# Pointwise product on split, masked h; the last two boxes on VectorE; x3 in one buffer

## The chip, the cores and the metric

The kernel runs on one core of a Trainium2 chip. The metric is device time in microseconds for one execution of the whole program; smaller is better. A core has five engines that run their own instruction streams side by side: TensorE (PE), VectorE (DVE), ScalarE (ACT), GpSimd (POOL) and SyncE (SP), which here only starts DMAs. They wait for each other through semaphores.

## What is computed

Thirty-two images of 256 channels and 28 x 28 positions go through four residual layers, all in fp32 at the interface:

```
x = x + L0(_gn(x))   # mixture of 8 pointwise convolutions, weights by sparsemax of a gate
x = x + L1(_gn(x))   # depthwise 3x3, batch norm, relu, prune; pointwise, batch norm, relu, prune
x = x + L2(_gn(x))   # attention over tokens with squared, normalised q and k
x = x + L3(_gn(x))   # 3x3 box filter with weights 1/9
```

`_gn` is a group norm with 32 groups. The part that the change touches first is in L1: after the depthwise convolution `h = _prune(h, 4.0)` sets a whole channel of an image to zero when its largest value is below 4, and then the pointwise product `pw_w @ h` mixes the 256 channels. The part touched second is L3: each output position is x3 plus the sum over its 3 x 3 neighbourhood of the normalised x3 (scaled by 1/9, zero outside the image).

## The kernel before

The 256 channels lie as J = 2 halves of 128 partitions; one half of an image is a tile 128 x 784. The program is a software pipeline over images. `run` calls each engine's `step(t)` for t = -1 to 36 (t = 8 to 29 as a hardware loop of pairs), and in a step seven images are in work at once, named by their stage: Z = t+1 (load), A = t (layer 0), B = t-1 (depthwise), C_ = t-2 (prune and pointwise), D = t-3 (queries, keys), E = t-4 (attention out, x3), F = t-5 (box). Order within a step is written out by hand for each engine; it is the order of calls in that engine's `step`. All waits are on semaphores counted per image. A full step, with every stage active, is one period of the pipeline; there are 28 steps from t = 4 to t = 31 that end with an image in stage A.

The order on **PE** in a step is: `value_out(E)`, key norms, `attention_weights(E)` (L503, L506), `gate_logits(A)` (L448), `attention_out(E)` (24 products of L457), `mix_experts(A)` (L585), `keys(D)` (L536, L539), `queries(D)` (24 of L457), transposes (L471), `pointwise(C_)` (8 of L457), `query_sums` (L555), `mixed_conv(A)` (L598), `query_scales` (L567), `keys_x` (L610), `key_sums` (L484), `group_means` (L441). The helper `conv_tile` issues all 128 x 392 products from L457. Products on two "parts" use a split: a value is stored as a rounded fp32r high part and the fp32r remainder, and `by_parts` multiplies high by high, high by low and low by high, so three products stand for one. `pointwise` doesn't use the split: it multiplies plain fp32 `pw_masked` by plain fp32 `h`.

The order on **ACT** around the change: relu of the depthwise result (`relu_h`, L1097), split of xn2, `sum_over_h` (L1106, which finds whether a channel reaches 4), `normalise_x3(F)` (L1013), `scaled_mix(A)` (L1029, waits for `mix_experts`), the second `sum_over_h`, then `square_k` (L1133, seven tiles) interleaved with four sums over the next input (`x0_sum`, L1042), `square_q` (L1142), `copy_tokens` (L1059), `fourth_powers_q` (L1151), `relu_y` and `sum_over_y` (L1123, L1115), `q_norms` (L1158), the sums of squares (L992), `q_high` (L1050) and `kx_high` (L1164).

The order on **DVE**: group norm scales, `q_low(E)` (L858), one depthwise tap, `attention_weights_low(E)` (L871), the sparsemax, `x2_low(D)` (L878), `make_x3(E)` (L840), two taps, `h_mask(C_)` (L811), `box_row_sums(F)` (L851, L853), `reciprocal_sums(D)` (L884, waits for all of `square_k`), nine taps (L803), `q_scales(D)` (L895, waits for `q_norms`), `make_x2`, `make_x1`, `scale_q`, the last six taps, `kx_low`.

**POOL** normalises x1 into `xpad` (L1256), and then `mask_weights` (L1280) multiplies the pointwise weights by the image's channel mask; PE's `pointwise` waits for that. Then `add_rows(F)` adds the box to the result in memory: SP has stored x3 of the image to `out`, and POOL issues three DMAs that accumulate `row_sums`, shifted by 0, 1 and 2 rows, into it, one after the other:

```
for n in range(BOX_ROWS):
    if n:
        pool.wait_ge(rows_added[n - 1].of(F), rows_added[n - 1].at(F))
    rows = row_sums[:, :, n:n + H, :].rearrange("p j h w -> p j (h w)")
    pool.dma_start(out_dram[F.times(1)], rows, accum_op=ALU.add).then_inc(rows_added[n].of(F), 16)
```

`box_row_sums(F)` overwrites `row_sums` and so waits for the DMAs of the image before. x3 has two buffers, so `make_x3(E)` waits for the store and the normalising of the image two before.

Of the kernel before, what the change touches and what calls it, by code (L numbers as in the profile page):

```python
# [5 lines left out]
ALU = mybir.AluOpType  # L6
# [6 lines left out]
P = 128  # L13
# [19 lines left out]
STAGES = 7  # L33

# [15 lines left out]
class Image:  # L50
# [21 lines left out]
    @property  # L72
    def active(self):

        return self.pair is not None or 0 <= self.offset < IMAGES

# [36 lines left out]
def build(nc, x, gate_wT, gate_b, expert_rows, mix_pattern, dw_w, channel_params, pw_wT, w_qk, b_qk, w_vT, w_ln, group_mean, ident, out):  # L113
    with ExitStack() as ctx:
# [18 lines left out]
        pw_sb = sb("pw_sb", [P, J, C])  # L133
# [24 lines left out]
        pw_masked = sb("pw_masked", [P, J, C])  # L158
# [12 lines left out]
        q_parts = sb("q_parts", [P, 2, J, HW], F32R)  # L171
        x3 = sb("x3", [P, 2, J, HW])
# [4 lines left out]
        wqk_raw = x3[:, 0].rearrange("p j n -> p (j n)")[:, 0:J * 2 * C].rearrange("p (j n) -> p j n", j=J)  # L177
        wv_ln = x3[:, 1].rearrange("p j n -> p (j n)")[:, 0:2 * J * C].rearrange("p (w j n) -> p w j n", w=2, j=J)
# [80 lines left out]
        pw_masked_ready = sig("pw_masked_ready", J)  # L259
# [40 lines left out]
        row_step = sig("row_step", 2)  # L300

# [10 lines left out]
        def row_operands(n):  # L312
# [5 lines left out]
                    (sums, sums, x3pad[:, :, 1:1 + H, 2:2 + W])][n]  # L318

# [3 lines left out]
        def run(eng, step):  # L323
# [32 lines left out]
            (pw_sb[:], pw_wT.rearrange("(j p) o -> p j o", p=P)),  # L356
# [5 lines left out]
        def _(sp):  # L362
# [9 lines left out]
            def step(t):  # L372
                Z, E = t + 1, t - 4
# [11 lines left out]
            for last in (Image(None, IMAGES - 2), Image(None, IMAGES - 1)):  # L385
# [6 lines left out]
        def _(pe):  # L392
# [261 lines left out]
        def _(dve):  # L654
# [15 lines left out]
            def setup_weights():  # L670
# [25 lines left out]
                for n, (bn, bias) in enumerate(((bn1_sb, dwb_sb), (bn2_sb, pwb_sb))):  # L696
# [4 lines left out]
                    did(nc.vector.tensor_tensor(bn_shift[:, n, :], bn_tmp[:, n, :], bn[:, 1, :], ALU.add))  # L701
                parts_of(wqk, wqk_raw)
# [85 lines left out]
            def depthwise(B, turns):  # L788

                for j, tap in TAP_TURNS[turns]:  # L790
                    if tap == 0:
                        dve.wait_ge(xpad_ready.sem, xpad_ready.at(B, j + 1))
                        if (B - 2).active:
                            dve.wait_ge(pw_mm.sem, pw_mm.at(B - 2))
# [11 lines left out]
            def h_mask(C_):  # L806

                dve.wait_ge(h_over_sum.sem, h_over_sum.at(C_))
                if (C_ - 1).active:
                    dve.wait_ge(pw_masked_ready.sem, pw_masked_ready.at(C_ - 1))  # L810
                nc.vector.tensor_scalar(hmask[:], h_over[:], 0.0, None, ALU.is_gt).then_inc(hmask_step.sem, 1)  # L811

# [534 lines left out]
```

## Time and profile before

| | us |
|---|---|
| median of 3 runs (lowest to highest) | 1646.85 (1644.88 to 1647.62) |
| the profiled execution, its own time | 1646.53 |
| its span in the trace | 1644.9 |
| PE busy | 1517.3 (92%) |
| DVE busy | 1296.9 (79%) |
| ACT busy | 1186.2 (72%) |
| POOL busy | 304.0 (18%) |

The span is what the trace covers; the 1.6 us between it and the execution's own time lie around the program. "Busy" counts only work, not waits. An engine's share is an average over the filling of the pipeline (to about 145 us), the full steps (to about 1446 us) and the draining. In the trace's rows a number behind "idle" or in square brackets is the time that the engine stood still just before the instruction, with what ended it. PE and PEld are TensorE's products and its weight loads, which overlap.

### The profile page before, as it was taken

Reading aid. Unit: us, or ns where it says so; the run is one execution under the profiler, and the core shown is the slowest. Engines: PE = TensorE matmul, PEld = TensorE weight load, DVE = VectorE, ACT = ScalarE, POOL = GpSimd, SP = SyncE. Lnnn points to the kernel's source line nnn. Section 1 sums busy time; section 2 is a strip of 40 time slices with the busy share of each in tenths; the row PEclk is TensorE's granted clock in tenths of the full one; section 3 lists DMA queues with packets and bytes.
Section 4 is the critical chain, followed back from the end, with each engine's and each line's share of the span. In section 5 each row is a group of like instructions: output and inputs, shape, how many; then the busy total and the mean of one; then the engine's idle time right before and its main releaser. Section 6 shows DMA issues by size and latency. Waiting matters only on the chain.

```text
span 1644.9 us, 27605 instructions
## 1 busy us (share of the span) xinstructions
PE 1517.3 (92%) x9282; PEld 1219.7 (74%) x9282; DVE 1296.9 (79%) x2339; ACT 1186.2 (72%) x2440; POOL 304.0 (18%) x238
## 2 busy tenths in 40 slices
PE   4469999999999999999999999999999999999850
PEld 2247787888887877878887877888877878878750
DVE  5758888888988888888888888889888888885430
ACT  3357777887777778877787778877787778776530
POOL 1100022222221121222221221222211221211001
PEclk8679999999999999999999999999999999999975
DMA  4001044434334444433334444333434444333435
GB/s 144 22 20 40 21 99 99 98 62 94 82 80 95 78 98 98 82 74 86 89 79 90 86 98 98 73 84 78 89 87 78 98 98 79 67 72 67 80 72 96
DMA packets 47172, 132.70 MB, mean 81 GB/s; under 512 B 3857, under 2 KB 4881, under 8 KB 47122
## 3 DMA queue, kind: packets, MB, share of 16 engines
q0 software_dynamic: 26112, 77.08, 28.8%
q1 hardware_dynamic: 20914, 54.98, 8.8%
q8 instruction: 28, 0.46, 0.1%
q14 instruction: 22, 0.18, 0.0%
q10 hardware_dynamic: 96, 0.00, 0.0%
HBM read 29.29 MB, written 102.76 MB: 80 GB/s over the span
## 4 chain that ended last, share of the span: by engine, by line
PE 90%; DVE 4%; DMA 2%; ACT 2%; issue 1%; POOLq 0%; ACTq 0%; DVEq 0%
PE conv_ps L457 35%; PE tile_ps L610 12%; PE tile_ps L539 10%; PE conv_ps L598 9%; PE small_ps L585 4%; PE tile_ps L484 4%; PE tile_ps L471 3%; PE tile_ps L567 3%; PE tile_ps L506 3%; DMA out<-row_sums 2%; PE tile_ps L503 2%; PE tile_ps L536 2%; PE tile_ps L555 2%; DVE h L803 1%; PE small_ps L448 1%
## 5 line engine op out<-in xcount | busy, mean ns | idle before, releaser
L803 DVE SCALAR_TENSOR_TENSOR h<-xpad,dw_sb,h 128x784 f32<-128x784 f32 x512 | 492.5, 1029 | 0.0
L1270 POOL DMA_DIRECT2D out<-row_sums x96 | 115.6, 1204 | 491.9 <-DMA out<-row_sums 411.2
L610 PE MATMUL tile_ps<-k,xT 112*128 112x256 f32 x896 | 201.4, 383 | 0.0
L1280 POOL TENSOR_SCALAR pw_masked<-pw_sb,hmask 128x256 f32<-128x256 f32 x64 | 118.4, 1857 | 385.4 <-DVE hmask L811 377.0
L610 PEld LDWEIGHTS tile_ps<-k,xT 112*128 112x128 f32 x896 | 171.9, 193 | 22.2
L539 PE MATMUL tile_ps<-wqk,xn_parts 128*112 128x256 f32 x1344 | 187.4, 294 | 0.0
L992 ACT ACTIVATE junk<-x 128x784 bf16<-128x784 f32 x192 | 162.8, 851 | 26.7 <-DVE x L830 17.5
L457 PE MATMUL conv_ps<-h,pw_masked 128*128 128x392 f32 x512 | 176.3, 498 | 5.5 <-issue 5.5
L598 PE MATMUL conv_ps<-x,mixed 128*128 128x392 f32 (+1 forms) x512 | 176.5, 498 | 2.2 <-ACT mixed L1029 1.1
L539 PEld LDWEIGHTS tile_ps<-wqk,xn_parts 128*112 128x112 f32 x1344 | 169.5, 175 | 0.1
L457 PE MATMUL conv_ps<-xn_parts,w_out 128*128 128x392 f32 x768 | 151.0, 345 | 0.0
L1256 POOL TENSOR_SCALAR xpad<-x,gn_rs 128x784 f32<-128x784 f32 x64 | 64.4, 1008 | 455.2 <-DVE gn_rs L727 455.2
L457 PEld LDWEIGHTS conv_ps<-h,pw_masked 128*128 128x128 f32 x512 | 96.1, 193 | 70.6 <-issue 9.4
L598 PEld LDWEIGHTS conv_ps<-x,mixed 128*128 128x128 f32 x512 | 95.8, 192 | 68.9 <-issue 6.6
L457 PE MATMUL conv_ps<-q_parts,attn_parts 128*128 128x392 f32 x768 | 145.3, 345 | 0.0
L457 PE MATMUL conv_ps<-xn_parts,wqk 128*128 128x392 f32 x768 | 142.7, 341 | 0.0
L457 PEld LDWEIGHTS conv_ps<-q_parts,attn_parts 128*128 128x128 f32 x768 | 135.9, 188 | 0.4 <-DVE attn_parts L871 0.3
L457 PEld LDWEIGHTS conv_ps<-xn_parts,wqk 128*128 128x128 f32 x768 | 135.7, 188 | 0.0
L457 PEld LDWEIGHTS conv_ps<-xn_parts,w_out 128*128 128x128 f32 x768 | 134.5, 188 | 0.0
L1042 ACT ACTIVATE junk<-x 128x784 bf16<-128x784 f32 x128 | 109.2, 854 | 1.1 <-issue 1.1
L1142 ACT ACTIVATE q<-conv_ps,bq_col 128x784 f32<-128x784 f32 x64 | 58.6, 915 | 50.4 <-PE conv_ps L457 50.2
L1133 ACT ACTIVATE k<-tile_ps 112x256 f32<-112x256 f32 x224 | 84.2, 381 | 8.0 <-PE tile_ps L539 7.9
(141 smaller groups left out, 2631.8 us busy)
## 6 DMA issues: line engine op xcount, KB each, us to landing
out<-row_sums POOLq DMA_DIRECT2D x96, 784.0 KB, 7.1
x<-x SPq DMA_DIRECT2D x32, 784.0 KB, 5.5
out<-x SPq DMA_DIRECT2D x32, 784.0 KB, 3.5
expert_sb<-expert_rows SPq DMA_DIRECT2D x8, 256.0 KB, 5.1
x<-w_qk SPq DMA_DIRECT2D x1, 512.0 KB
x<-w_vT SPq DMA_DIRECT2D x1, 256.0 KB
x<-w_ln SPq DMA_DIRECT2D x1, 256.0 KB
pw_sb<-pw_wT SPq DMA_DIRECT2D x1, 256.0 KB
```

Source lines behind the costliest of these rows:

```text
L457: mm = nc.tensor.matmul(conv_ps[:, 2 * j + a, 0:HALF], wt[:, half(j)], act[:, a * HALF:(a + 1) * HALF], start=(first and i == 0), stop=(la ...
L484: mm = nc.tensor.matmul(tile_ps[strip * SUB:(strip + 1) * SUB, KSUM_BANK, cols], weight.to_broadcast([TOK, SUB]), keys[:, m, :], start=(m ...
L539: mm = nc.tensor.matmul(dst, xn2_parts[:, u, i, m * TOK:(m + 1) * TOK], wqk[:, v, i, C:2 * C], start=False, stop=(i == J - 1 and u == 1))
L585: mm = nc.tensor.matmul(small_ps[s * SUB:(s + 1) * SUB, :], mix_w[:, g, :], expert_sb[:, g, s, :], start=(g == 0), stop=(g == PACKED - 1), ...
L598: mm = nc.tensor.matmul(conv_ps[:, 2 * j + a, 0:HALF + more], mixed[:, i * C + j * P:i * C + (j + 1) * P], x0[:, A.odd, i, a * HALF:(a + 1 ...
L610: mm = nc.tensor.matmul(tile_ps[:, KX_BANK, i * C:(i + 1) * C], xT[:, m, half(i)], k2[:, m, :], start=(m == 0), stop=(m == M - 1))
L803: ins = nc.vector.scalar_tensor_tensor(acc, view, scalar, acc, ALU.mult, ALU.add)
L992: nc.scalar.activation(junk[:, j * HW:(j + 1) * HW], source[:, j, :], ACT.Square, accum_out=gn_in[:, layer, 2 + j:3 + j]).then_inc(gn_sums ...
L1042: nc.scalar.activation(junk[:, j * HW:(j + 1) * HW], x0[:, Z.odd, j, 0:HW], func, accum_out=gn_in[:, 0, first + j:first + j + 1]).then_inc ...
L1133: nc.scalar.activation(k2[:, m, :], tile_ps[0:TOK, K_BANK[m // 2], m % 2 * C:(m % 2 + 1) * C], ACT.Square, accum_out=k_sum[:, m:m + 1]).th ...
L1270: pool.dma_start(out_dram[F.times(1)], rows, accum_op=ALU.add).then_inc(rows_added[n].of(F), 16)
L1280: nc.gpsimd.tensor_scalar(pw_masked[:, j, :], pw_sb[:, j, :], hmask[:, j:j + 1], 0.0, ALU.mult, ALU.add).then_inc(pw_masked_ready.sem, 1)
```

## The change

The pointwise product now goes by parts. The weights `pw_parts` are split once, in the setup on DVE (two more operations of `parts_of`). For each image ACT's new `h_high` makes the masked high part of h, and DVE's new `h_low` the masked remainder; POOL's `mask_weights` is gone. The parts of h live in the buffer that held those of q. In the last two images (`TAIL = 2`) the box is added on DVE by `box_in_tail` and stored by SP, half by half, in place of the store and the three accumulating DMAs. x3 is one buffer; x3 of the last image lies in x1's buffer. `normalise_x3` moves ahead of the first `sum_over_h` on ACT.

```diff
@@ SP, step
-                if E.active:
+                if E.active and not E.in_tail:
                     sp.wait_ge(x3_ready.sem, x3_ready.at(E))
-                    sp.dma_start(out_dram[E.times(1)], x3[:, E.odd]).then_inc(stored.of(E), 16)
+                    sp.dma_start(out_dram[E.times(1)], x3[:]).then_inc(stored.of(E), 16)
+                if F.in_tail:
+                    for j in range(J):
+                        sp.wait_ge(tail_step.sem, tail_step.at(F - (IMAGES - TAIL), 5 * (j + 1)))
+                        sp.dma_start(out_dram[F.offset][:, j, :], x3_of(F)[:, j, :]).then_inc(tail_stored, 16)
@@ PE
             def pointwise(C_, halves):
-                pe.wait_ge(h_ready.sem, h_ready.at(C_))
-                pe.wait_ge(pw_masked_ready.sem, pw_masked_ready.at(C_))
+                pe.wait_ge(h_lo.sem, h_lo.at(C_))
                 for j in halves:
                     wait_free((C_ - 1, q2_ready, j + 1), (C_ + 1, x1_ready, j + 1))
-                    conv_tile(j, [(pw_masked[:, i, :], h[:, C_.odd, i, :]) for i in range(J)]).then_inc(pw_mm.sem, 1)
+                    conv_tile(j, by_parts(pw_parts, h_parts)).then_inc(pw_mm.sem, 1)
@@ DVE
+                parts_of(pw_parts, pw_raw)
                 parts_of(wqk, wqk_raw)
...
+            def h_low(C_):
+                for j in range(J):
+                    dve.wait_ge(h_hi.sem, h_hi.at(C_, j + 1))
+                    nc.vector.scalar_tensor_tensor(h_parts[:, 1, j, :], h[:, C_.odd, j, :], hmask[:, j:j + 1],
+                                                   h_parts[:, 0, j, :].bitcast(F32), ALU.mult,
+                                                   ALU.subtract).then_inc(h_lo.sem, 1)
...
             def make_x3(E):
-                if (E - 2).active:
-                    dve.wait_ge(stored.of(E - 2), stored.at(E - 2))
-                    dve.wait_ge(x3pad_ready.sem, x3pad_ready.at(E - 2))
+                if (E - 1).active and not (E - 1).in_tail:
+                    dve.wait_ge(stored.of(E - 1), stored.at(E - 1))
                 for j in range(J):
+                    if (E - 1).active:
+                        dve.wait_ge(x3pad_ready.sem, x3pad_ready.at(E - 1, j + 1))
                     dve.wait_ge(attn_mm.sem, attn_mm.at(E, j + 1))
...
+            def box_in_tail(F):
+                s, turn = tail_step, F - (IMAGES - TAIL)
+                for rows in rows_added:
+                    last = Image(None, IMAGES - TAIL - 1)
+                    dve.wait_ge(rows.of(last), rows.at(last))
+                for j in range(J):
+                    pad, rows, done = x3pad[:, j], row_sums[:, j], 5 * j
+                    inner, out = pad[:, 1:1 + H, 1:1 + W], x3_of(F)[:, j, :]
+                    dve.wait_ge(x3pad_ready.sem, x3pad_ready.at(F, j + 1))
...
@@ DVE, step
                 if C_.active:
                     h_mask(C_)
-                if F.active:
+                if F.in_tail:
+                    box_in_tail(F)
+                elif F.active:
                     box_row_sums(F)
+                if C_.active:
+                    h_low(C_)
@@ ACT
+            def h_high(C_):
+                act.wait_ge(hmask_step.sem, hmask_step.at(C_))
+                if (C_ - 2).active:
+                    act.wait_ge(attn_mm.sem, attn_mm.at(C_ - 2))
+                for j in range(J):
+                    nc.scalar.activation(h_parts[:, 0, j, :], h[:, C_.odd, j, :], ACT.Identity,
+                                         scale=hmask[:, j:j + 1]).then_inc(h_hi.sem, 1)
@@ ACT, step
-                if C_.active:
-                    sum_over_h(C_, 0)
                 if F.active:
                     normalise_x3(F)
                 if C_.active:
+                    sum_over_h(C_, 0)
                     relu_h(C_, 1)
...
                     sum_over_h(C_, 1)
+                    h_high(C_)
@@ POOL, step
-                if C_.active:
-                    mask_weights(C_)
-                if F.active:
+                if F.active and not F.in_tail:
                     add_rows(F)
```

The five operations of `box_in_tail` for a half are left plus middle column, plus right column (both into `row_sums`), upper plus middle row, plus lower row (both into the padded tile), and x3 plus that sum; each waits for the one before.

How the instructions of ACT stand in a full step of the loop, from the relu of the second half of h on. Names are tiles: `over,h_over` is the sum of `sum_over_h`, `mixed` the scaled expert weights, `hq_parts` the new parts of h, `k,k_sum` the squared keys, `junk,gn_in` a sum over the input. Before:

```order
L1097 ACTIVATE h<-h,bn_shift,bn_scale 128x784
L1029 ACTIVATE mixed<-small_ps,gn_rs 128x256 x2
L1105 REGISTER_ALU
L1106 ACTIVATE over,h_over<-h,below 128x784
L1132 REGISTER_ALU
L1133 ACTIVATE k,k_sum<-tile_ps 112x256 x2
```

With the change:

```order
L1157 ACTIVATE h<-h,bn_shift,bn_scale 128x784
L1087 ACTIVATE mixed<-small_ps,gn_rs 128x256 x2
L1165 REGISTER_ALU
L1166 ACTIVATE over,h_over<-h,below 128x784
L1171 REGISTER_ALU
L1175 ACTIVATE hq_parts<-h,hmask 128x784 x2
L1201 REGISTER_ALU
L1202 ACTIVATE k,k_sum<-tile_ps 112x256 x2
```

Two operations on 128 x 784 now stand between the second sum over h and the first squared key, behind a wait for DVE's mask.

The end of DVE's stream, from x3 of the last image (`x,gn_in<-conv_ps,b_out,x`) on. Before:

```order
L840 SCALAR_TENSOR_TENSOR x,gn_in<-conv_ps,b_out,x 128x784 x2
L851 TENSOR_TENSOR row_sums<-x3pad 128x2x784
L853 TENSOR_TENSOR row_sums<-row_sums,x3pad 128x2x784
L713 COPY gn_avg<-small_ps 128x16
```

With the change:

```order
L871 SCALAR_TENSOR_TENSOR x,gn_in<-conv_ps,b_out,x 128x784 x2
L885 TENSOR_TENSOR row_sums<-x3pad 128x784
L887 TENSOR_TENSOR row_sums<-row_sums,x3pad 128x784
L890 TENSOR_TENSOR x3pad<-row_sums 128x28x28
L892 TENSOR_TENSOR x3pad<-x3pad,row_sums 128x28x28
L894 TENSOR_TENSOR x<-x,x3pad 128x784
```

The five rows stand twice for image 30, and twice again for image 31 behind the group norm's last rows; the two whole-image row sums of each of these images are gone.

## Rows read from the trace of the kernel before

**Rows 1.** Busy time by engine in a stretch of full steps; columns as in the heading.

```profile
core 0: us, PE busy (x) PEld busy (x) DVE busy (x) ACT busy (x) POOL busy (x), PEclk, DMA share, GB/s
440.00:1000.00 560.00, 560.00 (x3491) 453.14 (x3490) 481.76 (x854) 445.06 (x921) 116.86 (x86) 1.00 0.40 87
```

**Rows 2.** The chain that ended last: start us, duration us, what.

```profile
144.89 0.33 PE small_ps L441 x2
...
710.22 4.42 PE conv_ps L457 x24
...
722.35 4.30 PE conv_ps L457 x24
...
727.96 5.27 PE conv_ps L457 x16
...
1445.82 0.33 PE small_ps L441 x2
```

**Rows 3.** Timeline of DVE and of PE's weight loads where `attention_out` begins.

```profile
755.58 0.87 DVE L871 SCALAR_TENSOR_TENSOR attn_parts<-tile_ps,k_inv,attn_parts 128x256 fp32r<-128x256 f32 x2
...
756.52 0.19 PEld L457 LDWEIGHTS conv_ps<-q_parts,attn_parts 128*128 128x128 f32 x1
```

**Rows 4.** Timeline of ACT in one full step.

```profile
718.31 0.38 ACT L1133 ACTIVATE k<-tile_ps 112x256 f32<-112x256 f32 x1
...
724.59 0.92 ACT L1142 ACTIVATE q<-conv_ps,bq_col 128x784 f32<-128x784 f32 x1 [0.21 <-PE conv_ps L457]
726.69 0.91 ACT L1142 ACTIVATE q<-conv_ps,bq_col 128x784 f32<-128x784 f32 x1 [1.18 <-PE conv_ps L457]
727.50 2.29 ACT L1059 ACTIVATE xT<-tile_ps,k_rec 112x256 f32<-112x256 f32 x6
...
735.75 0.32 ACT L1158 ACTIVATE q_norm<-tile_ps 128x196 f32<-128x196 f32 x1
```

**Rows 5.** Timeline of DVE in the same step.

```profile
718.41 0.17 DVE L811 TENSOR_SCALAR hmask<-h_over 128x2 f32<-128x2 f32 x1 [0.43 <-ACT over L1106]
...
724.42 0.17 DVE L884 TENSOR_SCALAR k_eps<-k_sum 112x7 f32<-112x7 f32 x1 [1.94 <-ACT k L1133]
...
736.10 0.27 DVE L895 TENSOR_SCALAR q_alpha<-q_norm 128x196 f32<-128x196 f32 x1 [2.56 <-ACT q_norm L1158]
```

**Rows 6.** Groups by line and shape, ACT, 300 to 1400 us: busy, mean ns.

```profile
L998 ACT ACTIVATE xn<-x,gn_rs 128x784 f32<-128x784 f32 x46 | 45.5, 1036 | 0.7
...
L1092 ACT CAST xn_parts<-xn 128x784 fp32r<-128x784 f32 x46 | 36.7, 845 | 10.1 <-PE conv_ps L457 10.1
```

**Rows 7.** The page's group of depthwise taps on DVE.

```profile
L803 DVE SCALAR_TENSOR_TENSOR h<-xpad,dw_sb,h 128x784 f32<-128x784 f32 x512 | 492.5, 1029 | 0.0
```

**Rows 8.** Timeline of DVE, ACT and POOL in the drain.

```profile
1454.25 1.86 DVE L878 TENSOR_TENSOR xn_parts<-xn,xn_parts 128x784 fp32r<-128x784 f32 x2 [1.03 <-ACT xn_parts L1092]
...
1589.69 0.08 DVE L840 DVE_READ_ACCUMULATOR x<-conv_ps,b_out,x 128x1 f32 x1
...
1593.22 0.16 DVE L713 COPY gn_avg<-small_ps 128x16 f32<-128x16 f32 x1
...
1594.76 1.97 ACT L1013 ACTIVATE x3pad<-x,box_rs 128x784 f32<-128x784 f32 x2 [0.73 <-DVE box_rs L735]
...
1635.95 1.20 POOL L1270 DMA_DIRECT2D out<-row_sums  x1 [6.29 <-DMA out<-row_sums]
```

**Rows 9.** DMA issues on the page: count, KB each, us to landing.

```profile
out<-row_sums POOLq DMA_DIRECT2D x96, 784.0 KB, 7.1
...
out<-x SPq DMA_DIRECT2D x32, 784.0 KB, 3.5
```

**Rows 10.** Timeline of DVE in the setup.

```profile
31.38 0.69 DVE L665 CAST wqk<-x 128x1024 fp32r<-128x1024 f32 x1
32.11 1.23 DVE L666 TENSOR_TENSOR wqk<-x,wqk 128x1024 fp32r<-128x1024 f32 x1
```

**Rows 11.** Timeline of PE and POOL in the fill, at the first pointwise product.

```profile
77.30 3.12 POOL L1280 TENSOR_SCALAR pw_masked<-pw_sb,hmask 128x256 f32<-128x256 f32 x2 [8.45 <-issue]
...
80.52 7.88 PE L457 MATMUL conv_ps<-h,pw_masked 128*128 128x392 f32 x16 [5.49 <-issue]
```

**Rows 12.** Timeline of PE in the drain, two waits of the same length.

```profile
1479.02 2.98 PE L567 MATMUL tile_ps<-q_alpha,idn 128*128 128x196 f32 x8 [3.44 <-DVE q_alpha L900]
...
1524.26 1.59 PE L567 MATMUL tile_ps<-q_alpha,idn 128*128 128x196 f32 x8 [3.44 <-DVE q_alpha L900]
```

More of the change, by code:

```diff
@@ L75, in active, with in_tail @@
         return self.pair is not None or 0 <= self.offset < IMAGES
+    @property
+    def in_tail(self):
+        return self.pair is None and IMAGES - TAIL <= self.offset < IMAGES
     @property
@@ L318, in row_operands, with x3_of, image_rows @@
                     (sums, sums, x3pad[:, :, 1:1 + H, 2:2 + W])][n]
+        def x3_of(E):
+            return x1[:, E.odd] if E.pair is None and E.offset == IMAGES - 1 else x3[:]
+        def image_rows(tile):
+            return tile.rearrange("p (h w) -> p h w", w=W)
         def conv_banks(j):
@@ L378, in step @@
                     sp.dma_start(x0[:, Z.odd, :, 0:HW], x_dram[Z.times(1)]).then_inc(x_loaded.of(Z), 16)
-                if E.active:
+                if E.active and not E.in_tail:
                     sp.wait_ge(x3_ready.sem, x3_ready.at(E))
                     hold(sp, "sp")
-                    sp.dma_start(out_dram[E.times(1)], x3[:, E.odd]).then_inc(stored.of(E), 16)
+                    sp.dma_start(out_dram[E.times(1)], x3[:]).then_inc(stored.of(E), 16)
[3 more added lines that the diff above has]
+                        sp.dma_start(out_dram[F.offset][:, j, :], x3_of(F)[:, j, :]).then_inc(tail_stored, 16)
             run(sp, step)
-            for last in (Image(None, IMAGES - 2), Image(None, IMAGES - 1)):
+            sp.wait_ge(tail_stored, 16 * J * TAIL)
+            for last in (Image(None, IMAGES - TAIL - 2), Image(None, IMAGES - TAIL - 1)):
                 sp.wait_ge(stored.of(last), stored.at(last))
@@ L1007, in normalise_x3 @@
             def normalise_x3(F):
[L1009 removed]
+                if (F - 1).in_tail:
+                    act.wait_ge(tail_step.sem, tail_step.at(F - 1 - (IMAGES - TAIL)))
+                elif (F - 1).active:
                     act.wait_ge(row_step.sem, row_step.at(F - 1))
@@ L1012, in normalise_x3 @@
                 for j in range(J):
-                    nc.scalar.activation(x3pad[:, j, 1:1 + H, 1:1 + W], x3[:, F.odd, j, :].rearrange("p (h w) -> p h w", w=W),
+                    nc.scalar.activation(x3pad[:, j, 1:1 + H, 1:1 + W], image_rows(x3_of(F)[:, j, :]),
                                          ACT.Identity, bias=box_rs[:, 1, j:j + 1],
@@ L1270, in add_rows @@
                     pool.dma_start(out_dram[F.times(1)], rows, accum_op=ALU.add).then_inc(rows_added[n].of(F), 16)
-            def mask_weights(C_):
-                if (C_ - 1).active:
-                    pool.wait_ge(pw_mm.sem, pw_mm.at(C_ - 1))
-                pool.wait_ge(w_loaded, LOADED)
-                pool.wait_ge(hmask_step.sem, hmask_step.at(C_))
-                hold(pool, "pool")
-                for j in range(J):
-                    nc.gpsimd.tensor_scalar(pw_masked[:, j, :], pw_sb[:, j, :], hmask[:, j:j + 1], 0.0, ALU.mult,
-                                            ALU.add).then_inc(pw_masked_ready.sem, 1)
             def step(t):
```

52 lines of the change are left out of this document (34 added, 18 removed).

## The prediction

> **What bounds the kernel now.** I read the table of stretches first. In the full steps PE is busy all the time, 560.00 of 560.00 us, at full clock [rows 1]. The chain of waits agrees: group means end the fill at 144.89 and the last full step at 1445.82, with nothing but PE between them [rows 2]. That is 1300.93 us for 28 steps, 46.46 each. So at first sight a cheaper product on PE is worth its full price in each step.
>
> The timeline where `attention_out` begins says otherwise. DVE finishes the low part of the attention weights at 755.58 + 0.87 = 756.45, and PE loads the first of them at 756.52, with no idle time reported [rows 3]. PE comes there just as its input does. Followed back, that input comes from a second loop. PE's queries end at 722.35 + 4.30 = 726.65 [rows 2]; ACT's second `square_q` starts at 726.69 after a wait of 1.18 [rows 4]; from there ACT works to `q_norms` at 735.75 [rows 4], DVE waits 2.56 for it and starts at 736.10 [rows 5], and from there DVE works, with gaps of a few tenths at most, to 756.45. Then PE goes through attention, expert mix, keys and queries again. This loop over ACT and DVE is as long as PE's own work, with at most 0.07 us to spare. Whatever PE saves outside it, as the pointwise product does, turns into a wait at `attention_out`; whatever ACT gains in work inside it lengthens the step.
>
> The second place is the end. DVE has x3 of the last image at 1589.77 [rows 8], and 55 us follow, up to 1644.9, in which six accumulating DMAs of some 7.1 us each [rows 9] run one after another.
>
> **The full steps.** The pointwise product takes 5.27 us; the queries, the same 24 products by parts that it becomes, take 4.30 [rows 2]. PE's own work falls by 0.97 a step. By the above it buys nothing here.
>
> `h_high` goes into ACT's stream between the second `sum_over_h` and the first `square_k`. It needs the mask, which DVE makes from that very sum: DVE starts it at 718.41 and has it at 718.58 [rows 5]. With 0.03 for the signal ACT starts at 718.61, where it starts `square_k` at 718.31 now [rows 4]: 0.30 lost. The two operations are not in this trace. Each reads one per-partition operand. A copy with none into fp32r takes 845 ns, an activation with two takes 1036 [rows 6]; I take the middle, 940, as one operand lies between none and two. Neighbours on ACT overlap by 0.10 (726.69 + 0.91 ends after the 727.50 at which the next starts [rows 4]), so the pair holds ACT for 2 x 0.84 = 1.68, between 1.49 and 1.87. ACT is late by 0.30 + 1.68 = 1.98.
>
> What it can give back is its wait for q: 0.21 and 1.18 [rows 4], with the overlap of 0.10 at each, 1.59. So `copy_tokens` and all behind it, `q_norms` too, start 0.39 later (0.20 to 0.58). Nothing behind has slack: DVE waits for `q_norms`, and from there the loop is full. Each full step grows by 0.39; the 0.07 to spare is left out as a bound. **28 x 0.39 = +10.9** (+3.6 to +16.2).
>
> `h_low` is two three-operand operations of 1029 ns [rows 7] on DVE behind the row sums. It lies in the 1.94 us for which DVE waits for the squared keys [rows 5], and that wait grows by the 1.98 that ACT is late. So it costs nothing; without the cover it would be 2.0 a step. The nine taps behind start about 2.3 later, and have 2.56 before `q_norms` [rows 5] plus the 0.39. PE wants the parts of h at 727.96 [rows 2]; the row sums end at 724.42 - 1.94 = 722.5 [rows 5], so h_low ends near 724.5. POOL's `mask_weights` hid behind queries and transposes, and its removal gives nothing in full steps.
>
> One buffer for x3: `make_x3` of E now needs the store of the image before, issued a whole step earlier and landed in 3.5 us [rows 9], and its normalising, which moves ahead of a sum on ACT and was there in time already. Nothing. SP and POOL queue nothing more behind it.
>
> **The fill.** Setup gains a cast and a difference on 512 columns, on DVE's critical stretch. On 1024 they take 0.69 and 1.23 [rows 10]; half is 0.96, **+1.0**. In step 2 the chain passes the mask. POOL works on it for 3.12 us, and PE starts at 80.52 and needs 7.88, much of it at half clock [rows 11]. Now two operations on ACT and one more on DVE stand there, about 2.7, and the product falls by near a fifth; DVE gets the nine taps later, which takes part back. I put **-1.5** (0 to -3). In step 3, already PE's, but before the loop closes, the 0.97 counts once: **-1.0**. The drain is ACT's chain, and h_high there lies before PE's queries end: 0.
>
> **The tail.** From 1589.77: image 30's box is ten operations on 128 x 784. Two differences of that size take 1.86 [rows 8], 0.93 each; with a wait each, 0.95, 9.5. The group norm follows, 1593.22 to 1594.76 now, 1.5, and the first half of the normalising, 1.0 of 1.97 [rows 8]. Image 31's box is 9.5 more. The store of the last half: 3.5 for 784 KB [rows 9], I take 3.0. Now the last DMA is issued at 1635.95 [rows 8], lands after 7.1, at 1643.0, and the program ends 1.9 later; I keep the 1.9. 1589.8 + 9.5 + 1.5 + 1.0 + 9.5 + 3.0 + 1.9 = 1616.2, against 1644.9: **-28.7** (-26 to -31).
>
> **Sum:** +10.9 + 1.0 - 1.5 - 1.0 - 28.7 = -19.3, from the profiled 1646.53 to **1627** (1.2% less). The median of the runs shown is 0.3 above the profiled execution, which changes nothing. About 0.2%, 3.3 us, is what a measurement can tell from no change.
>
> **Rivals.**
> 1. *The loop has slack that the rows don't show, and PE stays the bound.* Then each step falls by 0.97 in place of growing by 0.39: 28 x 1.36 = 38 less, 1589. For it: PE never shows idle time in 560 us [rows 1]. Against: 0.07 us between DVE's end and PE's load [rows 3]. In between, if h_high hides wholly, the step stays and the time is 1616. Chances 0.04 and 0.10.
> 2. *The clock falls at the new wait (slower).* PE will stand still before `attention_out` in each step, by 0.97 + 0.39 = 1.4 us. In the drain PE stood for 3.44 us twice; once the four products behind ran at half clock, 2.98 us, and once near full speed, 1.59 [rows 12]. If the shorter wait did it too, `attention_out`, 4.42 us [rows 2] and inside the loop, would double: 28 x 4.4 = 123, 1750. From about five such steps in 28 it outweighs the gain. Against: 1.4 is under half of a wait that drops the clock only sometimes. The Trainium skill (TensorE: Matmul & The Clock Gate, "A second HAM failure mode: psum-queue depth-cycling") says that frequent small idles between groups of products can make the clock swing between its levels; by that rule the time would be this rival's. Chance 0.04.
> 3. *ACT's pair is far dearer, or another input of PE comes late as well.* The gain is used up if a step grows by 0.39 + 19.3 / 28 = 1.08. The pair would have to hold ACT for 2.4 us, over the 1.87 of the dearest row. ACT's delay also reaches other groups of PE (transposes, `query_scales`), but a short wait there would only use up time in which PE stands anyway. Chance 0.07, at 1640 to 1655.
> 4. *The tail gains less.* If the boxes' operations took 1.3 us, or row sums of image 29 were late, it would be -20: 1636. In the forecast's range.
>
> **How the numbers follow.** Forecast 0.75, rival 1 with its middle case 0.14, rival 2 0.04, rival 3 0.07. The bounds of the terms give 1617 to 1636; toward 1616 and 1640 they take in the middle case and part of rival 3: 1615 to 1640. Faster by over 0.2%: 0.88; within 0.2%: 0.05 (part of rival 3); slower: 0.07.
>
> **What would show it.** Right: group means 46.8 to 46.9 apart in full steps; PE idle about 1.4 us before the first weights of `attention_out`, released by DVE's low part; ACT no longer waiting before q; `hq_parts` on ACT at 0.94; the pointwise products at 4.3; 25 us from x3 of the last image to the end. Wrong: a step at 45.5, or the granted clock under 1.00 in the full steps, or a step over 47.2 with a wait at another of PE's groups.

## The result, and the profile after

| | us |
|---|---|
| before, median of 4 runs (lowest to highest) | 1647.23 (1644.88 to 1648.14) |
| after, median of 4 runs (lowest to highest) | 1622.07 (1621.39 to 1622.87) |
| after / before | 0.985 (0.983 to 0.987) |
| span of the profiled execution, before, after | 1644.9, 1620.0 |
| forecast | 1627 (1615 to 1640) |

The change makes the kernel 1.5% faster. All of that, and more, comes from the last two boxes; the split product costs a little.

The page of the changed kernel, its first and fourth part:

```profile
PE 1489.3 (92%) x9538; PEld 1262.6 (78%) x9538; DVE 1363.8 (84%) x2421; ACT 1225.7 (76%) x2504; POOL 180.2 (11%) x168
...
ACT 34%; DVE 33%; issue 20%; PE 11%; ACTq 1%; DVEq 0%; DMA 0%
```

PE's busy time fell by 28 us, and the chain that ended last is now ACT and DVE in turn, where before it was PE for 90% of the span. This is the change of bound that the first two parts of the forecast argue for: before, PE's work and the loop over ACT and DVE were of nearly the same length (46.46 and 46.31 us, as the experiments show), and the chain could be read either way.

The same stretch of full steps as in [rows 1]:

```profile
core 0: us, PE busy (x) PEld busy (x) DVE busy (x) ACT busy (x) POOL busy (x), PEclk, DMA share, GB/s
440.00:1000.00 560.00, 547.80 (x3569) 466.57 (x3569) 499.44 (x878) 456.94 (x937) 67.14 (x60) 1.00 0.40 86
```

PE now stands still for 12.2 of 560 us, at a granted clock of 1.00 throughout. The timeline of PE shows where, once in each step:

```profile
749.14 0.40 PE L463 MATMUL small_ps<-gn_in,gmean 128*128 128x16 f32 x2
...
757.99 4.54 PE L479 MATMUL conv_ps<-hq_parts,attn_parts 128*128 128x392 f32 x24 [0.98 <-DVE attn_parts L923]
...
775.60 4.54 PE L479 MATMUL conv_ps<-hq_parts,pw_parts 128*128 128x392 f32 x24
```

It waits before `attention_out` for DVE's low part of the attention weights, as in [rows 3], only that the wait is open now. The timeline of ACT in that step answers to [rows 4]:

```profile
766.50 1.79 ACT L1175 ACTIVATE hq_parts<-h,hmask 128x784 fp32r<-128x784 f32 x2 [0.24 <-DVE hmask L833]
768.19 0.36 ACT L1202 ACTIVATE k<-tile_ps 112x256 f32<-112x256 f32 x1
...
774.05 1.75 ACT L1211 ACTIVATE q<-conv_ps,bq_col 128x784 f32<-128x784 f32 x2
775.64 2.33 ACT L1119 ACTIVATE xT<-tile_ps,k_rec 112x256 f32<-112x256 f32 x6
...
783.83 0.32 ACT L1227 ACTIVATE q_norm<-tile_ps 128x196 f32<-128x196 f32 x1
```

The pair of `h_high` holds ACT from 766.50 to 768.19, 1.69 us. The two waits for q, 0.21 and 1.18 before, are gone: both halves run back to back. DVE in the same step, for [rows 5]:

```profile
770.03 1.98 DVE L839 SCALAR_TENSOR_TENSOR hq_parts<-h,hmask,hq_parts 128x784 fp32r<-128x784 f32 x2
774.21 0.17 DVE L936 TENSOR_SCALAR k_eps<-k_sum 112x7 f32<-112x7 f32 x1 [2.20 <-ACT k L1202]
774.74 8.60 DVE L825 SCALAR_TENSOR_TENSOR h<-xpad,dw_sb,h 128x784 f32<-128x784 f32 x9
784.19 0.26 DVE L947 TENSOR_SCALAR q_alpha<-q_norm 128x196 f32<-128x196 f32 x1 [0.85 <-ACT q_norm L1227]
```

`h_low` lies in DVE's wait for the squared keys, and 2.20 us of that wait are left behind it.

The tail, in the timeline of DVE and ACT, for [rows 8]:

```profile
1594.67 0.08 DVE L871 DVE_READ_ACCUMULATOR x<-conv_ps,b_out,x 128x1 f32 x1
1594.67 0.97 DVE L885 TENSOR_TENSOR row_sums<-x3pad 128x784 f32<-128x784 f32 x1
...
1604.53 0.17 DVE L735 COPY gn_avg<-small_ps 128x16 f32<-128x16 f32 x1
...
1606.07 1.98 ACT L1071 ACTIVATE x3pad<-x,box_rs 128x784 f32<-128x784 f32 x2 [0.73 <-DVE box_rs L757]
1607.24 0.97 DVE L885 TENSOR_TENSOR row_sums<-x3pad 128x784 f32<-128x784 f32 x1 [1.27 <-ACT x3pad L1071]
...
1616.21 0.98 DVE L894 TENSOR_TENSOR x<-x,x3pad 128x784 f32<-128x784 f32 x1
```

From the end of x3 of the last image, 1594.75, to the end of the span there are 25.2 us, where there were 55.1.

The whole can be cut at the group means. Fill: to the group means of step 3 (144.82 before, by the timeline's row; 143.67 after). Full steps: to those of step 31 (1445.75; 1448.62). Drain: to the last (1590.90; 1595.88). Tail: the rest.

| stretch | before | after | difference | forecast |
|---|---|---|---|---|
| fill | 144.8 | 143.7 | -1.1 | -1.5 |
| 28 full steps | 1300.9 | 1304.9 | +4.0 | +10.9 |
| drain | 145.2 | 147.3 | +2.1 | 0 |
| tail | 54.0 | 24.1 | -29.9 | -28.7 |
| sum | 1644.9 | 1620.0 | -24.9 | -19.3 |

The row of the fill is the least certain. It ends at 144.8 to 146.4 in the four traces with the whole old product (before, tail only, one buffer alone, two sums moved before the change), and at 143.2 to 145.4 in the seven with the split product and no work added: about 1.9 less in the mean.

### The profile page after: what moved, and what is told of

Read it like the earlier page. It is cut to its first block, busy times and chain, and to the rows that moved or that the text cites. A ratio compares the mean times of both kernels' runs of the same rounds, so it can differ in the third digit from the quotient of the medians.

```text
span 1620.0 us, 28154 instructions
## 1 busy us (share of the span) xinstructions
PE 1489.3 (92%) x9538; PEld 1262.6 (78%) x9538; DVE 1363.8 (84%) x2421; ACT 1225.7 (76%) x2504; POOL 180.2 (11%) x168
## 4 chain that ended last, share of the span: by engine, by line
ACT 34%; DVE 33%; issue 20%; PE 11%; ACTq 1%; DVEq 0%; DMA 0%
DVE h L825 9%; ACT junk L1100 6%; PE conv_ps L479 5%; ACT xT L1119 5%; ACT k L1202 3%; DVE hq_parts L910 3%; DVE x L851 3%; ACT x L1192 3%; ACT over L1166 3%; ACT x3pad L1071 3%; DVE q L959 3%; DVE x L860 3%; ACT fourth L1220 2%; ACT hq_parts L1175 2%; ACT h L1157 2%
## 5 line engine op out<-in xcount | busy, mean ns | idle before, releaser
L1339 POOL DMA_DIRECT2D out<-row_sums x90 | 108.4, 1205 | 895.4 <-DVE row_sums L905 468.4
L479 PE MATMUL conv_ps<-hq_parts,attn_parts 128*128 128x392 f32 x768 | 145.2, 344 | 27.9 <-DVE attn_parts L923 27.9
L479 PEld LDWEIGHTS conv_ps<-hq_parts,attn_parts 128*128 128x128 f32 x768 | 135.4, 188 | 30.8 <-DVE attn_parts L923 30.7
L479 PE MATMUL conv_ps<-hq_parts,pw_parts 128*128 128x392 f32 x768 | 147.2, 347 | 5.1 <-DVE hq_parts L839 5.1
L479 PEld LDWEIGHTS conv_ps<-hq_parts,pw_parts 128*128 128x128 f32 x768 | 137.5, 191 | 6.5 <-DVE hq_parts L839 6.5
L1087 ACT ACTIVATE mixed<-small_ps,gn_rs 128x256 f32<-128x256 f32 x64 | 26.8, 472 | 104.0 <-issue 87.2
L1119 ACT ACTIVATE xT<-tile_ps,k_rec 112x256 f32<-112x256 f32 x224 | 88.9, 514 | 1.9 <-PE tile_ps L493 1.9
```

The source lines that it names most:

```text
L479: mm = nc.tensor.matmul(conv_ps[:, 2 * j + a, 0:HALF], wt[:, half(j)], act[:, a * HALF:(a + 1) * HALF], start=(first and i == 0), stop=(la ...
L1119: nc.scalar.activation(xT[:, m, :], tile_ps[0:TOK, XT_BANK[m // 2], m % 2 * C:(m % 2 + 1) * C], ACT.Identity, scale=k_rec[:, m:m + 1]).the ...
```

## The experiments

The theory: in full steps a loop runs over PE (attention to queries), ACT (q to the root of the norms) and DVE (from there to the attention weights), and was as long as PE's own work; so PE's saving buys nothing, ACT's addition lengthens the step, and only the tail gives time. The rivals: PE was the bound and the split product saved its 0.97 a step; or the one buffer of x3 costs something of its own. Each time is compared with runs of the kernel before on the same chip, whose medians were 1646.6 to 1647.2. "A step" below is the distance of the group means of step 31 and step 4 over 27: 46.46 before, 46.62 after.

### The parts alone

**Tail only.** The change with the fp32 product and GpSimd's masked weights put back:

```diff
...
-                    conv_tile(j, by_parts(pw_parts, h_parts)).then_inc(pw_mm.sem, 1)
+                    conv_tile(j, [(pw_masked[:, i, :], h[:, C_.odd, i, :]) for i in range(J)]).then_inc(pw_mm.sem, 1)
...
-                if C_.active:
-                    h_low(C_)
...
-                    h_high(C_)
...
+                if C_.active:
+                    mask_weights(C_)
```

> The change without its pointwise part: fp32 weights masked on GpSimd as before, but the boxes of the last two images on VectorE and x3 in one buffer. My theory (a loop over ScalarE and VectorE is as long as TensorE's step, so the split buys nothing in full steps and costs a little in the drain): the tail gives 30 us and nothing else moves, 1617 us, faster than the whole change (1622). Rival (the split product saves its 0.97 us of TensorE in each step and the tail gives nothing): 1647.

Measured: 1616.05 us, ratio 0.981 (0.979 to 0.983), step 46.47. The theory's 1617; and 6 us faster than the whole change.

**Split only.** The change with `TAIL = 0`, so that all boxes are added by DMAs:

```diff
-TAIL = 2
+TAIL = 0
...
-            return x1[:, E.odd] if E.pair is None and E.offset == IMAGES - 1 else x3[:]
+            return x3[:]
...
-            sp.wait_ge(tail_stored, 16 * J * TAIL)
```

> The change without its tail: split product and one x3 buffer, all boxes by accumulating DMAs. My theory: -1.2 us in the fill, +4 in the full steps, +2 in the drain, as the two traces show: 1652 us, slower than before. Rival (the product's saving counts): 1620.

Measured: 1651.59 us, ratio 1.0027 (1.0017 to 1.0037), step 46.63. The split product (with the one buffer) makes the kernel slower by 4.4 us, though PE's work in it is less.

**One buffer for x3 alone:** both of these edits together.

> Only x3 in one buffer, with the normalising of x3 ahead of the first sum over h on ScalarE; product and boxes as before. My theory: no wait appears, 1647 us within 1.5. Rival (one buffer makes the making of x3 wait for the store or the normalising): a wait of some tenths of a microsecond in each step, 1652 or more.

Measured: 1646.64 us, ratio 0.9995 (0.9986 to 1.0005): no difference. The three parts add up: -31.2 for tail and buffer and +4.4 for split and buffer, less the -0.6 of the buffer that both contain, are about -26, and the whole change measured -25.2.

### What bounds the full step

**Half of the product left out**, in the kernel before. The sum over the second half of the input channels is not computed:

```diff
-                    conv_tile(j, [(pw_masked[:, i, :], h[:, C_.odd, i, :]) for i in range(J)]).then_inc(pw_mm.sem, 1)
+                    conv_tile(j, [(pw_masked[:, 0, :], h[:, C_.odd, 0, :])]).then_inc(pw_mm.sem, 1)
```

> The kernel before with half of the pointwise product left out (one half of the input channels), so 2.6 us less work on TensorE in each step. My theory: the loop over ScalarE and VectorE holds the step at 46.4, TensorE stands still 2.6 us before the attention product, and the time falls only in the fill: 1643 us (1640 to 1646). Rival (TensorE bounds the full steps alone): 28 x 2.6 = 74 us less, 1573.

Measured: 1644.07 us, ratio 0.9981 (0.9972 to 0.9991); the step is 46.43 in the mean. The timeline of PE in two full steps, the second with the clock lost:

```profile
704.12 4.54 PE L457 MATMUL conv_ps<-q_parts,attn_parts 128*128 128x392 f32 x24 [1.46 <-DVE attn_parts L871]
...
725.35 0.87 PE L555 MATMUL tile_ps<-fourth,ones 128*32 128x196 f32 x16 [0.74 <-ACT fourth L1151]
...
796.81 6.11 PE L457 MATMUL conv_ps<-q_parts,attn_parts 128*128 128x392 f32 x24 [1.46 <-DVE attn_parts L871]
```

2.6 us less work on an engine that was busy 560.00 of 560.00 us shorten the step by 0.03 in the mean. 2.20 of it stands in the two waits of 1.46 and 0.74, one for DVE and one for ACT. But the mean hides something. Two of the 28 steps took 47.94: behind the wait of 1.46 the granted clock was 0.67 from 796.80 to 800.00, and `attention_out` took 6.11 in place of 4.54. The others took 46.16 to 46.37. The loop with its clock kept is 46.31, so the slack was about 0.15, not 0.03. That PE "never idles" said little of what its work was worth.

The full steps can be laid side by side from the first product of `attention_out` on. The table has medians over 25 of them; "moved" is the run of the two moved sums below.

| us after `attention_out` begins | before | half product | after | moved |
|---|---|---|---|---|
| first squared key (ACT) | 8.21 | 8.22 | 10.22 | 10.22 |
| second half of q (ACT) | 16.59 | 16.60 | 16.87 | 16.60 |
| root of the norms (ACT) | 25.65 | 25.55 | 25.86 | 25.55 |
| low part of the weights (DVE) | 45.50 | 45.39 | 45.70 | 45.40 |
| next `attention_out` (PE) | 46.46 | 46.31 | 46.62 | 46.32 |

Of the 0.15, 0.04 lay before `attention_out` (0.96 against 0.92 behind the start of DVE's low part), within the forecast's 0.07. The other 0.10 lay between q and the root, where the rows of before report no idle time:

```profile
727.79 5.43 PE L457 MATMUL conv_ps<-h,pw_masked 128*128 128x392 f32 x16
...
733.33 1.00 ACT L1123 ACTIVATE x<-conv_ps,bn_shift,bn_scale 128x784 f32<-128x784 f32 x1
```

The relu of the second half of y reads the pointwise product. It starts 0.11 behind the product's end (733.22), 0.10 later in its step than where the product is done early. So the pointwise product was not wholly outside the loop.

**More products**, in the changed kernel: four split products, 0.72 us, ahead of each pointwise product, their sums overwritten.

```diff
+                    conv_tile(j, by_parts(pw_parts, h_parts)[:1], last=False)
                     conv_tile(j, by_parts(pw_parts, h_parts)).then_inc(pw_mm.sem, 1)
```

> The changed kernel with four more split products in front of each pointwise product (their sums are overwritten), 0.72 us more work on TensorE in each step. My theory: TensorE stands still 0.98 us in each step, so they are hidden there and the wait shrinks to about 0.3; 1623 us (1622 to 1625; they show in fill only). Rival (TensorE's work sets the step): 1622 + 28 x 0.72 = 1642.

Measured: 1623.47 us, ratio 0.9863 (0.9846 to 0.9879); the step is 46.66. PE's timeline:

```profile
712.24 4.56 PE L479 MATMUL conv_ps<-hq_parts,attn_parts 128*128 128x392 f32 x24 [0.35 <-DVE attn_parts L924]
```

The wait gave 0.63 to 0.70 of the 0.72, and the time rose by 1.4.

**A third activation** in front of `h_high`'s pair:

```diff
+                nc.scalar.activation(h_parts[:, 1, 0, :], h[:, C_.odd, 0, :], ACT.Identity, scale=hmask[:, 0:1])
                 for j in range(J):
                     nc.scalar.activation(h_parts[:, 0, j, :], h[:, C_.odd, j, :], ACT.Identity,
```

> The changed kernel with one more masked activation on 128 x 784 in front of the pair on ScalarE (it is written where VectorE then puts the low part). It holds ScalarE for 0.84 us. My theory: its waits for q are used up, so each of the 28 full steps grows by all of 0.84, and fill and drain by 1 to 2: 1622 + 23.5 + 1.5 = 1647. Rival (there is still slack on ScalarE): 1622 to 1630.

Measured: 1651.47 us, ratio 1.0031 (1.0020 to 1.0041); the step is 47.56, 0.94 more. ACT's timeline:

```profile
779.87 0.95 ACT L1174 ACTIVATE hq_parts<-h,hmask 128x784 fp32r<-128x784 f32 x1 [0.23 <-DVE hmask L833]
780.73 1.78 ACT L1176 ACTIVATE hq_parts<-h,hmask 128x784 fp32r<-128x784 f32 x2
782.41 0.36 ACT L1203 ACTIVATE k<-tile_ps 112x256 f32<-112x256 f32 x1
```

It holds ACT for 0.86, and the step pays that in full and 0.08 more; the time is 4.5 above the 1647 that I expected. In one of the 28 steps the clock fell, as with half the product, and that step took 49.36, 1.9 more than its neighbours, or 0.07 a step:

```profile
1104.50 6.10 PE L479 MATMUL conv_ps<-hq_parts,attn_parts 128*128 128x392 f32 x24 [1.46 <-DVE attn_parts L923]
```

ACT has no slack left there, as said; in the change itself the slack took most of the pair's price.

### Which loop

**Two sums moved.** In the changed kernel two of the four sums over the next input go from between the squared keys to in front of the scaled expert weights, where ACT stood still 2.40 us:

```diff
+                if Z.active:
+                    for n in range(MOVED):
+                        x0_sum(Z, n)
                 if A.active:
                     scaled_mix(A)
...
-                    if Z.active and 0 < m <= 2 * J:
+                    if Z.active and MOVED < m <= 2 * J:
                         x0_sum(Z, m - 1)
```

> The changed kernel with the first two of the four sums over the next input moved on ScalarE: from between the squared keys to in front of the scaled expert weights, where ScalarE stands still 2.40 us. That takes 1.7 us out of the loop and leaves ScalarE's total work as it is. My theory: the loop falls to 44.9, TensorE's own 45.5 becomes the step, the granted wait at the attention product goes: 28 x 1.1 = 31 less, 1591 us. Rival (the step is set by ScalarE's or VectorE's total work, or by TensorE): 1622.

Measured: 1613.54 us, ratio 0.9801 (0.9784 to 0.9817); the step is 46.32. Neither: 8.5 us less, not 31 and not 0. ACT's timeline shows what I had overlooked:

```profile
769.23 0.92 ACT L1212 ACTIVATE q<-conv_ps,bq_col 128x784 f32<-128x784 f32 x1
771.32 0.92 ACT L1212 ACTIVATE q<-conv_ps,bq_col 128x784 f32<-128x784 f32 x1 [1.18 <-PE conv_ps L480]
```

The wait of 1.18 for the second half of q is back. There are two loops with a common part. One enters ACT by the expert mix and the squared keys, the other by the queries, and from q on both go the same way over ACT and DVE. The change made the first the longer one; the move shortens it, and the second takes over at 46.32, which is what it was before the change too (46.31 with half the product). I had even used it in the forecast, and then not in this expectation.

**The same move before the change**, where PE has work for all of 46.46:

> The same move in the kernel before, whose TensorE works all of its 46.46. My theory: loop and TensorE are equally long there, so relieving the loop alone gives nothing: 1647 us (1644 to 1648). Rival (the loop alone was the bound): up to 1600.

Measured: 1647.35 us, ratio 1.0006 (0.9996 to 1.0015), step 46.47: nothing, as expected. This tests less than I meant: before the change ACT still waited for q (0.21 and 1.18), so the loop through the squared keys was the shorter one, and the move relieves only that. The loop through the queries was not touched.

**The root early.** To shorten both loops, the common part must lose something. `q_norms`, for which DVE waits, stood behind both halves of relu and sum of y on ACT. In the step of the changed kernel shown above its input, PE's `query_sums`, is there at 780.93, and it starts at 783.83, 2.9 us later:

```diff
                     sum_over_y(C_, 0)
+                if D.active:
+                    q_norms(D)
+                if C_.active:
                     relu_y(C_, 1)
                     sum_over_y(C_, 1)
                 if D.active:
                     copy_tokens(D, range(6, M))
-                    q_norms(D)
```

> The changed kernel with the root of the query norms on ScalarE issued between the two halves of relu and sum of y, 2.1 us of ScalarE's work earlier, and nothing else. VectorE waits 0.85 us for it in each step and is then bound by its own nine taps. My theory (the loop over ScalarE and VectorE sets the step): each full step falls by 0.85 to 45.8, 28 x 0.85 = 24 less, 1598 us. Rival (after the run with moved sums: another chain, which doesn't pass the root, sets the step at 46.3 to 46.6): 1622.

Measured: 1586.91 us, ratio 0.9637 (0.9622 to 0.9652), 35 us less than the change and 11 less than expected. The step is 45.67, 0.95 less, or 26 us, where I had 24. The drain fell by 9.1 us, which I had not expected: each of its steps is such a chain. The timelines of DVE and then of PE's drain:

```profile
715.66 8.60 DVE L825 SCALAR_TENSOR_TENSOR h<-xpad,dw_sb,h 128x784 f32<-128x784 f32 x9
...
724.18 0.26 DVE L947 TENSOR_SCALAR q_alpha<-q_norm 128x196 f32<-128x196 f32 x1
```

```profile
1453.12 2.21 PE L588 MATMUL tile_ps<-q_alpha,idn 128*128 128x196 f32 x8 [1.90 <-DVE q_alpha L952]
...
1495.13 1.59 PE L588 MATMUL tile_ps<-q_alpha,idn 128*128 128x196 f32 x8 [1.91 <-DVE q_alpha L952]
```

DVE no longer waits: `q_scales` follows its taps directly. In the drain PE waits 1.90 and 1.91 for the query scales, where it waited 4.32 in the changed kernel.

**Both moves:**

> Both moves: two sums over the input in front of the scaled expert weights, and the root of the query norms early. My theory: the loop through the squared keys and the loop through the queries are both shorter than TensorE's own 45.5, which becomes the step: 28 x 1.1 = 31 less than the change, 1591 us, and only now does the split product give its 0.97 in each step. Rival (still a loop over VectorE): as the early root alone, 1598.

Measured: 1583.21 us, ratio 0.9615 (0.9600 to 0.9630), 8 less than expected; the 28 full steps gave 27.8 and the drain 10.9, which I had left out. The full steps:

```profile
core 0: us, PE busy (x) PEld busy (x) DVE busy (x) ACT busy (x) POOL busy (x), PEclk, DMA share, GB/s
440.00:1000.00 560.00, 560.00 (x3641) 475.69 (x3640) 515.01 (x893) 468.33 (x959) 68.32 (x61) 1.00 0.42 89
```

PE is busy throughout again, and the step is 45.62: 0.84 below the step before the change. That this is PE's own work agrees with the changed kernel, where PE's waits can be seen and taken off: it was busy 1277.63 us in the 28 full steps, 45.63 each. So the split product's saving was real, and shows once the loops are out of the way. No run took work off PE in this version, and none made both moves with the old product, so what the split is worth beside the moves is read from these rows and not measured.

### Drain and tail

**The drain's order.** In the drain's steps that have both, `h_high` comes behind the squared keys, and `h_low` behind `reciprocal_sums`:

```diff
...
                     sum_over_h(C_, 1)
-                    h_high(C_)
+                    if A.active or not D.active:
+                        h_high(C_)
...
+                if C_.active and D.active and not A.active:
+                    h_high(C_)
                 if D.active:
                     square_q(D)
```

> The changed kernel with the high part of h made behind the squared keys in the two drain steps that have both, as TensorE's keys stand still 0.41 to 0.63 us there for the second squared key. My theory: these waits go, 1 to 2 us less, 1620.5. Rival (ScalarE's chain takes it back later in the same step): 1622.

Measured: 1621.58 us, ratio 0.9845 (0.9832 to 0.9859), against 1622.07 and 0.9850 (0.9833 to 0.9867) for the change: not to be told from no change. The waits for the squared keys are gone from PE's timeline. The drain is 146.5 us in the profiled execution, 0.8 less than the change's 147.3, which the whole times can't confirm. The wait behind them stays as long:

```profile
1482.12 2.98 PE L588 MATMUL tile_ps<-q_alpha,idn 128*128 128x196 f32 x8 [4.31 <-DVE q_alpha L952]
1527.24 2.98 PE L588 MATMUL tile_ps<-q_alpha,idn 128*128 128x196 f32 x8 [4.31 <-DVE q_alpha L952]
```

So the small waits explain at most part of the +2.1. The same rows of the changed kernel show the larger part, in one step:

```profile
1482.98 2.98 PE L588 MATMUL tile_ps<-q_alpha,idn 128*128 128x196 f32 x8 [4.32 <-DVE q_alpha L952]
1512.06 0.32 PE L557 MATMUL tile_ps<-bqk,ones 128*112 128x256 bf16 x1 [0.20 <-ACT k L1202]
1528.47 2.98 PE L588 MATMUL tile_ps<-q_alpha,idn 128*128 128x196 f32 x8 [4.32 <-DVE q_alpha L952]
```

Before, PE waited 3.44 us at both places, and behind the second its four products took 1.59 [rows 12]. Now it gets there earlier by the 0.9 that the split product saves, waits 4.32, and the products take 2.98, at half clock. The table of stretches shows the clock behind the second wait:

```profile
1528.00:1532.00 4.00, 3.53 (x10) 0.50 0.32 31
1532.00:1538.00 6.00, 6.00 (x27) 0.92 0.64 120
```

That costs 1.4 us in the four products and some 0.8 in `keys_x` behind them (6.85 against 6.05 in the chains). It is the mechanism of my second rival, at a place where I didn't look for it. It is not the whole account: by the group means the first three steps of the drain changed by +1.0 (45.51 to 46.52), +2.5 (42.43 to 44.93) and -1.5 (43.19 to 41.70). In the first PE waits 0.55 for DVE's low part and 0.41 for a squared key; the second has the clock; in the third the products behind its waits ran faster than before (`keys_x` 6.34 in place of 7.41). So the +2.1 is a sum of larger terms of both signs.

**All together:** both moves, the drain's order, three of image 30's box operations in DVE's waits for x3 of image 31, and image 31 normalised into `xpad`, so that image 30's second half runs meanwhile:

```diff
                 for j in range(J):
+                    if (E - 1).in_tail:
+                        box_in_tail(E - 1, [range(2), range(2, 3)][j])
                     if (E - 1).active:
...
                 if F.in_tail:
-                    box_in_tail(F)
+                    if E.active:
+                        box_in_tail(F, range(3, 5))
+                    else:
+                        box_in_tail(F - 1, range(5, 10))
+                        box_in_tail(F)
```

> Both moves, the drain's order, and a tail in which three of image 30's ten box operations run in VectorE's waits for x3 of image 31 and image 31 is normalised into the buffer of layer 1, so that this overlaps with image 30's second half. My theory: 1591 - 1 for the drain - 3.0 - 1.2 for the tail = 1586 us. Rival (the tail's operations delay x3 of image 31 by as much): 1590.

Measured: 1579.88 us, ratio 0.9598 (0.9583 to 0.9612), 2.6% faster than the change and the fastest of all. It missed the expected time as both moves together had missed theirs: the early root is worth more than I wrote. Against the both-moves version the tail from the last group means is 19.7 in place of 24.1 us, 4.4 less where 4.2 was expected. The whole time is only 3.3 less, and the drain is 0.9 longer (137.3 against 136.4), with the clock lost behind a wait of 1.91 that kept it there:

```profile
1491.62 2.95 PE L593 MATMUL tile_ps<-q_alpha,idn 128*128 128x196 f32 x8 [1.91 <-DVE q_alpha L959]
```

The timeline of DVE in the tail:

```profile
1551.18 0.98 DVE L901 TENSOR_TENSOR row_sums<-x3pad 128x784 f32<-128x784 f32 x1 [0.16 <-ACT x3pad L1086]
1552.19 0.98 DVE L901 TENSOR_TENSOR row_sums<-row_sums,x3pad 128x784 f32<-128x784 f32 x1
1553.64 1.03 DVE L878 SCALAR_TENSOR_TENSOR x<-conv_ps,b_out,x 128x784 f32<-128x784 f32 x1 [0.47 <-PE conv_ps L484]
```

The first two operations stand in the wait for PE, which was 2.62 us long and is 0.47 now.

## Why the prediction was right, and where its sizes were off

- **The bound: right.** The step where the forecast turned, that a PE busy all the time buys nothing since its input at `attention_out` comes just in time, is shown by leaving out half the product (0.15 us a step for 2.6 us of work, and 0.03 in the mean with two steps at a lost clock) and by adding products (hidden). The slack before `attention_out`, which the forecast bounded by 0.07, was 0.04; another 0.10 lay where ACT's relu waited for the pointwise product, which the forecast had placed outside the loop.
- **h_high: mechanism right, size off.** Its pair held ACT for 1.69, forecast 1.68; one operation 945 ns, forecast 940. The term for the full steps was mis-sized in what ACT gives back. I counted its reported waits for q with the overlap, 1.59, and got 0.39 a step; measured are 0.13 in the step shown and 0.14 on average over the 28. By the medians in the table ACT is late by 2.01 at the first squared key (forecast 1.98) and by 0.28 at the second half of q: it gave back 1.73. Part of the difference stands in the block of squared keys, which took 5.59 us before (718.31 to 723.90) and 5.51 after (768.19 to 773.70); why is open. Another 0.07 came back between q and the root, where ACT no longer waits for the product, and 0.04 before `attention_out`. +10.9 was +4.0, near the lower bound of +3.6, and between the forecast and the case of rival 1 in which `h_high` hides wholly.
- **h_low: right.** In DVE's wait, at no cost, with 2.20 us of it left.
- **x3 in one buffer: right.** 0.9995 (0.9986 to 1.0005).
- **Fill: right, within its scatter.** In the two traces setup's operations put 1.38 us on the group means of step 0 (38.80 to 40.18), but traces with the same setup lie 0.8 to 1.0 apart there. By the means of the four and the seven traces named above, setup cost 0.9 (forecast 1.0), step 2 gave 2.1 (forecast 1.5) and step 3 gave 0.7 (forecast 1.0).
- **Drain: wrong.** "The drain is ACT's chain, and h_high there lies before PE's queries end: 0". It was +2.1. The term was put at nothing by following ACT alone. PE waits for a squared key behind `h_high` (0.41 and 0.20), and it comes 0.9 earlier to a wait behind which the clock was kept once and lost once, though I had the two rows [rows 12]; the second such wait went from 3.44 to 4.32 and cost 2.2 us of clock. That the longer wait is what lost the clock fits the other runs (3.44 there in four traces with the old product, kept each time; 3.62 or more in six with the changed one, lost each time), but no run changed the wait alone.
- **Tail: right.** The box operations took 0.98 and 1.01 from start to start, forecast 0.95; the stores of half an image landed in 2.4 us, forecast 3.0. -29.9 against -28.7.
- **Rival 1** fell: the hidden slack was 0.15, not the 0.97 and more that it needs. **Rival 2** fell for the full steps of the change, at a granted clock of 1.00 with PE idle 1.0 us in each, and came true once in the drain. Some luck is in that: the forecast had PE idle 1.4 us, and behind waits of 1.46 the clock fell in two of the nine full steps that had one with half the product, and in one of two with the third activation. Such a step cost 1.6 to 1.9 us, not the 4.4 that the forecast put on it. **Rival 3** fell.
- **The sum.** The time lies 5 us under the forecast. The full steps alone were 6.9 off; the drain's +2.1 took part of that back.

What stays open: whether the early root alone would speed up the kernel before. With PE's own work at 46.46 a step it should gain only in the drain; it was not tried.

## What to carry to other kernels

An engine that is busy all the time is not shown to be the bound; look at how long its inputs had been there when it took them, at the place where another engine's chain enters. Where two chains are nearly equally long, a saving on one is invisible until the other is shortened too, and a cheap way can be the order: one small operation, moved ahead of three larger ones, gave 35 us, more than the whole change. And read the steps one by one before taking their mean: two slow steps of 28 hid four fifths of the slack. The end of a program has its own bound, here a row of six dependent DMAs, and deserves its own sum.

## What the runs showed of the hardware that I had not expected

What TensorE's waits did to its clock, in full steps and drain. "Lost" means half clock behind the wait:

| wait | where | clock behind it |
|---|---|---|
| 0.5 to 1.1 | before `attention_out`, the change, all full steps | kept each time |
| up to 1.45 | the same, half product and third activation | kept each time |
| 1.46 | the same, 11 in both runs | lost 3 times |
| 1.9 | first two waits before `query_scales` in the drain, the three runs with the early root | kept 3 times (1.59 or 1.60 us for the four products), in part once (2.21), lost once (2.95) |
| 2.47 | the same, once | kept (1.59) |
| 3.44 | the same, the kernel before | lost at the first, kept at the second |
| 4.32 | the same, the change | lost at both |

So longer waits lost the clock more often, but the length doesn't decide it alone; what else does was not traced. The row-sum additions on DVE, L853, took 1950 ns with GpSimd's masking in the kernel; with that gone their successor took 1.79 us, and with the masking put back (tail only) 1.95 again.
